# Two heads in each half of TensorE's rows for the scores, and the heads' sums spread by VectorE's shuffle

## The reference, cut to what matters

```python
x = conv3x3(quantize(x), sign(W) * mean|W|) + b
qkv = layernorm(x) @ wqkv + bqkv                 # per image 49 regions of 64 pixels
q_reg, k_reg = q.mean(pixels), k.mean(pixels)
idx = top_k(q_reg @ k_reg.T, 4)                  # 4 regions for each region
scores = q[region, head] @ k[idx, head].T * scale    # 8 heads of 8: 64 x 256
out = softmax(scores) @ v[idx, head]
x = x + out @ wo + bo
x = x + gelu(layernorm(x) @ w1 + bm1) @ w2 + bm2
```

## Time and profile before

| | |
|---|---|
| median of 3 runs | 5610.56 us (5608.67 to 5612.54) |
| the profiled execution's own time | 5625.85 us |
| its span, first to last instruction | 5623.2 us |
| mean granted TensorE clock | 0.898 |
| TensorE busy | 4720.9 us |
| VectorE busy | 3648.9 us |
| ScalarE busy | 3287.3 us |
| GpSimd busy | 2777.4 us |

### The profile page before, as it was taken

The page is one execution under the profiler, slowest core; times in us unless marked ns, Lnnn a source line. Parts: engine busy times, 40 slices in busy tenths (PEclk is TensorE's granted clock), DMA queues, the critical chain, the costliest instruction groups (busy, mean ns, idle before and its releaser), DMA issues.

```text
span 5623.2 us, 182695 instructions
## 1 busy us (share of the span) xinstructions
PE 4720.9 (84%) x43666; PEld 3049.9 (54%) x43666; DVE 3648.9 (65%) x8855; ACT 3287.3 (58%) x6282; POOL 2777.4 (49%) x9656
## 2 busy tenths in 40 slices
PE   2388888888889898888888889888888888888888
PEld 1265555655556555555555556555565655556564
DVE  2266666766667666676766667666676766667676
ACT  1156556565665756556565665656556565665657
POOL 1245455454554645455454554545455464554553
PEclk9589899988889989898989999989899998999989
DMA  2333343333423334243333423334233333423311
GB/s 61 95 99 92 82 109 75 94 84 91 108 68 102 82 93 103 72 109 83 96 87 89 109 69 101 82 94 104 71 110 88 94 84 92 111 65 106 83 45 33
DMA packets 626961, 494.05 MB, mean 88 GB/s; under 512 B 483792, under 2 KB 613968, under 8 KB 615536
## 3 DMA queue, kind: packets, MB, share of 16 engines
q10 hardware_dynamic: 335360, 212.04, 16.6%
q1 hardware_dynamic: 290416, 268.94, 16.5%
HBM read 268.80 MB, written 211.94 MB: 85 GB/s over the span
## 4 chain that ended last, share of the span: by engine, by line
PE 52%; DMA 13%; issue 9%; ACT 7%; DVE 6%; DVEq 4%; SPq 4%; ACTq 3%; POOL 2%; POOLq 0%
PE ps L1003 11%; PE ps L1033 9%; PE ps L1017 8%; DMA max_d<-tr 6%; PE ps L896 5%; DMA qm<-qk_d 3%; DVEq L223 3%; PE ps L953 3%; ACTq L237 2%; PE ps L989 2%; PE ps L916 2%; PE ps L912 2%; DMA xin<-in_x 2%; ACT pt L847 2%; PE ps L974 2%
## 5 line engine op out<-in xcount | busy, mean ns | idle before, releaser
L736 DVE TENSOR_REDUCE mx<-ps 128x4 f32<-128x1024 f32 x1568 | 1921.6, 1225 | 1396.2 <-PE ps L1003 1128.7
L847 ACT ACTIVATE pt<-ps 128x512 f32<-128x512 f32 x3136 | 1694.2, 592 | 875.0 <-PE ps L1017 811.9
L505 POOL COPY vg<-vs 64x72 f32 x6272 | 1563.5, 249 | 781.6 <-POOL kg L490 576.7
L1003 PE MATMUL ps<-kg,qm 96*128 96x256 f32 x6272 | 1358.3, 342 | 364.4 <-DVE mx L736 112.2
L490 POOL CAST kg<-ks 96x128 fp32r x3136 | 845.2, 295 | 1550.5 <-PE ps L1017 1195.5
L1003 PEld LDWEIGHTS ps<-kg,qm 96*128 96x128 f32 x6272 | 963.3, 206 | 1087.2 <-issue 889.0
L1017 PE MATMUL ps<-qm,kg 97*128 97x256 f32 x6272 | 1126.5, 303 | 151.7 <-ACT pt L847 96.9
L1033 PE MATMUL ps<-pt,vg 128*32 128x128 f32 x25088 | 1092.0, 294 | 51.8 <-DVE um L726 39.1
L1017 PEld LDWEIGHTS ps<-qm,kg 97*128 97x128 f32 x6272 | 940.2, 206 | 214.6 <-ACT pt L847 154.7
L1033 PEld LDWEIGHTS ps<-pt,vg 128*32 128x32 f32 x25088 | 629.5, 114 | 296.5 <-issue 58.0
L645 DVE CAST kg<-ks 96x128 fp32r x3136 | 630.9, 244 | 137.9 <-issue 132.4
(11 more groups left out here) (113 smaller groups left out, 4036.1 us busy)
## 6 DMA issues: line engine op xcount, KB each, us to landing
qk_d<-stg SPq DMA_DIRECT2D x224, 448.0 KB, 3.6
qm<-qk_d ACTq DMA_DIRECT2D x1792, 42.0 KB
ks<-qk_d ACTq DMA_DIRECT2D x96, 784.0 KB, 6.3
vs<-v_d ACTq DMA_DIRECT2D x64, 882.0 KB, 7.1
xin<-in_x SPq DMA_DIRECT2D x119, 224.0 KB, 2.6
xi_d<-xi SPq DMA_DIRECT2D x112, 224.0 KB, 2.7
qk_d<-stg SPq DMA_DIRECT2D x112, 224.0 KB, 3.2
max_d<-tr SPq DMA_DIRECT2D x1568, 2.0 KB
```

The source lines that it names most:

```text
L505: j = pool.tensor_copy(vg[slot][rows, (k // 2) * VW:(k // 2 + 1) * VW], vs[place(m)[0]][rows, bass.ds(region, 1), :].rearrange("p o n -> p ...
L736: v.tensor_reduce(mx[h % 2][:].rearrange("p (g j e) -> p g j e", g=2, j=2)[:, :, :, 0], ps[:, 0:2, :].rearrange("p g (j k) -> p g j k", j= ...
L847: act.activation(pt[m % 2][:, c], ps[:, 2 + c, :], ACT.Exp, scale=float(HD) ** -0.5).then_inc(S["pt_ready"], 1)
L1003: i = pe.matmul(ps[:, g, 256 * j:256 * j + 256], qm[c % 2][0:NP3, t, g, 2 * j:2 * j + 2, :].rearrange("p h t -> p (h t)"), kg[slot][0:NP3, ...
```

## The change

`qm` and `ks`, and so `kg`, hold the heads 0 and 1 of a group in partitions 0 to 47 and heads 2 and 3 in partitions 64 to 111; row 48 of each half takes the maxima. `scores` is now four products of 48 rows, two in each half of the rows of the array, and the result's bank is that of the half. `turned` is eight products of 49 rows and 128 columns instead of four of 97 rows and 256 columns; it waits for both exponentials of the step before ahead of the first, and signals at the last two. The -1 rows are filled in `ks` at the start and come with the copies; the gathers copy 128 partitions instead of 96. The keys are loaded by six transfers instead of three, and the loads (eight with those of the values, before five) go out in consecutive steps instead of every second one. `pick` and its product are gone: VectorE shuffles `um` into `rc` at offsets 0 and 1 (`SPREAD` gives for each of 32 rows the row to take), and ScalarE takes the logarithm from `rc` instead of a bank. The waits on banks 5 and 6 move from offset 0 to offsets 4 and 9.

```diff
@@ -28,9 +28,12 @@
 EPS = 1e-5
 HG = 4
 NG = HEADS // HG
-NP3 = 3 * HG * HD
+HALF = 64
+NP3 = 3 * 2 * HD
 VC = 18
 VW = 4 * VC
+
+SPREAD = [16] * HD + [17] * HD + [16] * 16
@@ -49,7 +52,7 @@
 ROUTE_AT = 62
 A_LOAD, B_LOAD = 70, 6
 QK_DMAS, V_DMAS = 3, 4
-KV_DMAS = 5
+KV_DMAS = 8
@@ -141,7 +143,7 @@
         ks = [sb(f"ks{i}", [128, NG, R, RT], F32R) for i in range(2)]
         vs = [sb(f"vs{i}", [128, R, VW]) for i in range(2)]
-        qm = [sb(f"qm{i}", [128, NW, NG, HG, RT], F32R) for i in range(2)]
+        qm = [sb(f"qm{i}", [128, NW, NG, 2, RT], F32R) for i in range(2)]
         kg = [sb(f"kg{i}", [128, NG, TOPK, RT], F32R) for i in range(RING)]
         vg = [sb(f"vg{i}", [128, 2 * VW + 16]) for i in range(RING)]
@@ -234,16 +236,18 @@
             i, s = c // NW, c % NW
             src = qk_d[bass.ds(q, 1), i, 0:C, :, ST * s:ST * s + ST].rearrange("o (g h d) q (s t) -> g h (o d q) s t", g=NG, h=HG, s=NW)
             for g, h in heads:
-                eng.dma_start(qm[c % 2][24 * h:24 * h + 24, :, g, h, :].bitcast(F32), src[g, h]).then_inc(q_loaded[c % 2], 16)
+                row = HALF * (h // 2) + 24 * (h % 2)
+                eng.dma_start(qm[c % 2][row:row + 24, :, g, h % 2, :].bitcast(F32), src[g, h]).then_inc(q_loaded[c % 2], 16)
         def keys_values(eng, q, i, n):
-            if n < 3:
-                src = qk_d[bass.ds(q, 1), i, C:2 * C, n // 2, :].rearrange("o (g c) n -> (o c) g n", g=NG)
-                dst = ks[i][n:NP3:3].rearrange("p g r t -> p g (r t)").bitcast(F32)
+            if n < 6:
+                part, term = n // 3, n % 3
+                src = qk_d[bass.ds(q, 1), i, C:2 * C, term // 2, :].rearrange("o (g j c) n -> j (o c) g n", g=NG, j=2)[part]
+                dst = ks[i][HALF * part + term:HALF * part + NP3:3].rearrange("p g r t -> p g (r t)").bitcast(F32)
             else:
                 src = v_d[bass.ds(q, 1), i].rearrange("o t r n -> (o t) (r n)")
-                dst = vs[i][64 * (n - 3):64 * (n - 3) + 64].rearrange("p r n -> p (r n)")
+                dst = vs[i][64 * (n - 6):64 * (n - 6) + 64].rearrange("p r n -> p (r n)")
             eng.dma_start(dst, src).then_inc(kv_loaded[i], 16)
@@ -259,14 +263,14 @@
                 if h == A_LOAD:
                     staged_all(eng, p + 1)
                     gathered(eng, p, R)
-                if 0 <= h - A_LOAD < 2 * KV_DMAS and (h - A_LOAD) % 2 == 0:
-                    keys_values(eng, p + 1, 0, (h - A_LOAD) // 2)
+                if 0 <= h - A_LOAD < KV_DMAS:
+                    keys_values(eng, p + 1, 0, h - A_LOAD)
             local = h if kind == "lead" else h - STEPS
             if local >= 0 and kind != "last":
                 if local == B_LOAD and kind != "lead":
                     gathered(eng, p, STEPS)
-                if 0 <= local - B_LOAD < 2 * KV_DMAS and (local - B_LOAD) % 2 == 0:
-                    keys_values(eng, p if kind == "lead" else p + 1, 1, (local - B_LOAD) // 2)
+                if 0 <= local - B_LOAD < KV_DMAS:
+                    keys_values(eng, p if kind == "lead" else p + 1, 1, local - B_LOAD)
         def first_loads(eng):
@@ -361,8 +365,8 @@
                     sp.wait_ge(hopped[m % 2], (p * R + m // 2 + 1) * 16)
                     settled(sp)
-                    sp.dma_start(qm[m // NW % 2][NP3:NP3 + 1, m % NW].rearrange("o g h t -> o (g h t)").bitcast(F32),
-                                 max_d[m % RING].rearrange("j p -> (j p)").unsqueeze(0)).then_inc(row_ready[m % RING], 16)
+                    sp.dma_start(qm[m // NW % 2][NP3:128:HALF, m % NW].rearrange("o g e t -> o (g e t)").bitcast(F32),
+                                 max_d[m % RING].rearrange("(j g) p -> j (g p)", j=2)).then_inc(row_ready[m % RING], 16)
                 if live(h, kind):
...
@@ -487,8 +485,8 @@
                     pool.wait_ge(kv_loaded[i], (p + m // STEPS + 1) * (16 * KV_DMAS))
                     settled(pool)
                 for k, region in enumerate(chosen(m, 2)):
-                    j = pool.tensor_copy(kg[slot][0:NP3, :, 2 + k, :],
-                                         ks[place(m)[0]][0:NP3, :, bass.ds(region, 1), :].rearrange("p g o t -> p g (o t)"))
+                    j = pool.tensor_copy(kg[slot][:, :, 2 + k, :],
+                                         ks[place(m)[0]][:, :, bass.ds(region, 1), :].rearrange("p g o t -> p g (o t)"))
                 j.then_inc(S["kp_ready"], 1)
@@ -589,8 +587,8 @@
                 v.memset(t[:], 1.0)
             for t in qm:
                 v.memset(t[:].rearrange("p s g h t -> p (s g h t)").bitcast(F32), 0.0)
-            for t in kg:
-                v.memset(t[:].rearrange("p g k t -> p (g k t)").bitcast(F32), -1.0)
+            for t in ks:
+                v.memset(t[:].rearrange("p g r t -> p (g r t)").bitcast(F32), -1.0)
             link(v.memset(rx[:], 0.0))
             v.memset(epst, EPS)
@@ -642,8 +640,8 @@
                     settled(v)
                 gather_ready(v, p, m)
                 for k, region in enumerate(regions(v, regs, m, 0, 2)):
-                    j = v.tensor_copy(kg[slot][0:NP3, :, k, :],
-                                      ks[place(m)[0]][0:NP3, :, bass.ds(region, 1), :].rearrange("p g o t -> p g (o t)"))
+                    j = v.tensor_copy(kg[slot][:, :, k, :],
+                                      ks[place(m)[0]][:, :, bass.ds(region, 1), :].rearrange("p g o t -> p g (o t)"))
                 j.then_inc(S["kd_ready"], 1)
@@ -696,6 +694,11 @@
                 for s, off in f_item(h):
                     n = p * NW + s
                     b = s % 2
+                    if off in (0, 1):
+                        if off == 0:
+                            v.wait_ge(S["um_ready"], p * (4 * 14) + (NW + s + 1) * 4)
+                            settled(v)
+                        v.stream_shuffle(rc[:, off], um0[:, s] if off == 0 else um1[:, b], SPREAD).then_inc(S["sum_full"], 1)
                     if off in (2, 3):
                         i = off - 2
@@ -802,7 +805,7 @@
                     if off in (1, 2):
                         i = off - 1
                         act.wait_ge(S["sum_full"], n * 2 + i + 1)
-                        act.activation(rc[:, i], ps[:, 5 + i, 0:ST], ACT.Ln).then_inc(S["lns_ready"], 1)
+                        act.activation(rc[:, i], rc[:, i], ACT.Ln).then_inc(S["lns_ready"], 1)
                         act.wait_ge(S["lns_ready"], n * 2 + i + 1)
                         act.activation(rc[:, i], rc[:, i], ACT.Exp, scale=-1.0).then_inc(S["rcs_ready"], 1)
@@ -921,8 +924,6 @@
                 if h == ROUTE_AT:
                     pe.wait_ge(S["rx_ready"], q * NW + NW)
                     pe.wait_ge(S["l_ready"], q * (2 * NW) + 2 * NW)
-                    if not first:
-                        pe.wait_ge(S["lns_ready"], p * (2 * NW) + 1)
                     settled(pe)
                     for i in range(2):
@@ -940,21 +941,13 @@
                 for s, off in f_item(h):
                     n = p * NW + s
-                    if off == 0:
-                        pe.wait_ge(S["um_ready"], p * (4 * 14) + (NW + s + 1) * 4)
-                        if s >= 2:
-                            pe.wait_ge(S["ot_ready"], 1 + n - 1)
-                        elif kind == "loop":
-                            pe.wait_ge(S["l_ready"], (p + 2) * (2 * NW))
-                            pe.wait_ge(S["v_ready"], (p + 2) * NW)
-                        if s:
-                            pe.wait_ge(S["lnv2_ready"], n)
-                        for i, src in enumerate((um0[:, s], um1[:, s % 2])):
-                            pe.matmul(ps[:, 5 + i, 0:ST], pick[:], src, start=True, stop=True).then_inc(S["sum_full"], 1)
                     if off == 4:
                         pe.wait_ge(S["un_ready"], n * 2 + 2)
                         if s:
                             pe.wait_ge(S["z_ready"], n * 2)
+                        elif kind == "loop":
+                            pe.wait_ge(S["l_ready"], (p + 2) * (2 * NW))
+                            pe.wait_ge(S["v_ready"], (p + 2) * NW)
                         for i in range(2):
                             j = pe.matmul(ps[64 * i:64 * i + 64, 6, 0:ST], wo[:], rc[:, i], start=True, stop=True)
@@ -977,8 +970,9 @@
                         pe.matmul(ps[:, 6, 0:ST], mean_w[:], st2[:], start=True, stop=True).then_inc(S["var2_full"], 1)
                     if off == 9:
                         pe.wait_ge(S["nm2_ready"], n + 1)
-                        if s < NW - 1:
-                            pe.wait_ge(S["lns_ready"], n * 2 + 4)
+                        pe.wait_ge(S["ot_ready"], 1 + n)
+                        if s == 0 and kind == "loop":
+                            pe.wait_ge(S["lg_ready"], p + 2)
                         for i in range(2):
                             d = slice(64 * i, 64 * i + 64)
@@ -1000,9 +994,9 @@
                     pe.wait_ge(S["mx_ready"], T)
                 for g in range(NG):
                     for j in range(2):
```

(23 more changed lines are left out.)

13 lines of the change are left out of this document (3 added, 10 removed).

## The result

The changed kernel took **6002.18 us** (median of 4 runs, 5973.57 to 6031.92) beside 5611.55 us for the kernel before on the same chip: a ratio of 1.0692, 95% interval 1.0637 to 1.0746. It is slower by 6.9%. The forecast was 5645 us with a range of 5410 to 5830 us: the sign was right and the size far off. The profiled execution took 5973.57 us, with a span of 5971.7 us and a mean clock of 0.771 (0.898 before).

What follows compares the result with a forecast made beforehand. It took a ring of waits, scores, maximum, scores, as the bound, with no engine full. Gains of 204 us against 240 us of clock loss gave 5662 us profiled, so 5645 us predicted (+0.6%), range 5410 to 5830 us.

Steps and rivals of the forecast that it cites:

- a fall of the clock: TensorE drops to the lower clock after a less busy stretch; over two steps 3.2 us, of which 2.4 uncovered.
- the halves with their clock: Half-array products on TensorE: scores 0.24 us shorter per step, more at the lower clock, against a clock loss of 240 us.
- the late exponentials: Both exponentials start after all eight turned products; where ScalarE is late this costs 0.2 us, once per finishing cycle.
- finishing cycle: Steps that finish a strip, in a pattern repeating every 7 steps, 112 times over 16 pairs; forecast gain 0.16 us each.
- The eight loads: Loads of keys and values, eight instead of five with the same bytes: no time, covered by ScalarE's 42% idle.
- shuffle for the product: Two VectorE shuffles of 0.60 us replace TensorE's 1.77 us pick product per strip; VectorE ends last, so nothing of 1.77 is left.
- start: At the kernel's start, changed fills and the fills of the key ring together add 4 us.
- The clock, +240 us: Half of the finishing cycles and four tenths of the others fall once more: 112 x 0.9 x 2.4 us.
- The slot falls from 0.21 to about 0.12 us, 0.37 us less in a step: Turned products at the lower clock: time per product shrinks with half the columns; no gain at the upper clock.
- the -90 us: About 250 steps already at the lower clock save 0.80 us instead of 0.24, two thirds of the difference on the path.
- near 0.80: Sign that the forecast is right: TensorE's mean granted clock, 0.898 in the kernel before.
- TensorE's busy time: Sign that the forecast is right: total busy time of TensorE near 4300 us.

Runs made afterwards that it cites:

- all_but_halves: Kernel before with the shuffle, maxima written to two rows, turned products behind both exponentials and eight loads, without the array's halves: 5862.91 us, 1.0417.
- loads_spaced: Changed kernel with each pair of half loads of keys and values issued in one step, every second step: 5976.08 us, 1.0616.
- shuffle_only: Kernel before with only the product with pick replaced by VectorE's shuffles: 5572.87 us, 0.9912.
- late_exponentials: shuffle_only with full-height turned products that start behind both exponentials of the step before and give both signals at their end: 5682.57 us, 1.0095.
- one_row_and_fill: Changed kernel without the second half's row of maxima, with added TensorE products whose result nobody reads: 5750.22 us, 1.0238.
- split_on_sync: Changed kernel with the maxima written by two one-row transfers on SyncE's queue in place of one two-row transfer: 6078.13 us, 1.0812.

## Why the prediction was wrong

Three steps of the prediction failed most. It had no term for the row of maxima that becomes two (166 us, measured in full height). It priced a fall of the clock at 2.4 us, so that the halves with their clock came to about nothing (measured 154 us slower). And it took the late exponentials for 0.2 us once in a finishing cycle (22 us, measured 103 us). The eight loads, put at no time, cost 43 us.

The parts in order, in us against 5611.55; "measured" is the difference of two ratios of runs that differ in that part alone.

| part | forecast | measured |
|---|---|---|
| shuffle for the product | +13 | -49 |
| second row of maxima | not named | +166 |
| late exponentials | +22 | +103 |
| eight loads | 0 | +43 |
| these four together (all_but_halves) | +36 | +234 |
| the halves with their clock | about -4 | +154 |
| start | +4 | not taken apart |
| sum | +36 | +388 |

(The forecast's split: of a finishing cycle's 0.16 us, 0.48 is the scores, 0.2 the late exponentials; the rest, 0.12 x 112, is what the shuffle would cost.) The four parts measured one by one give 263 us, and together 234 us: their waits cover each other a little. And the 166 us are of full height with 4 KB; taken out of the changed kernel, the second row gives back 56 us, and 95 us with the idle products.

**The transfer that wasn't costed.** The largest single part has no term in the prediction. The change part by part left out that L364's one destination row becomes two. The line is in the diff, its duration was in the trace of before (0.23 us), and beside it stood a transfer to 16 partitions with 0.54 us in the same queue. These two were the bounds: up to 0.3 us in each of 1568 steps, some 490 us if all of it showed, on a chain of which `max_d<-tr` already held 6%.

**"Eight loads ... no time, covered by ScalarE's 42% idle".** The cover was looked for on the engine that issues. What grew is the wait for the maxima's transfer: from 251 to 310 us, and the longest from 4.3 to 10.2 us, in the full-height kernel that differs by these loads alone. The run changed three things at once, eight transfers for five, half the partitions in each of the key loads, and no step's pause between them. loads_spaced, which gives back the pause alone, took the longest wait from 10.5 to 6.6 us; that points at the pause and doesn't prove it.

**"This costs 0.2 us, once per finishing cycle".** The mechanism was right and the count was wrong: the prediction priced only the step in which ScalarE is late and TensorE waits. That wait did double (104 to 200 us in the waits of shuffle_only and late_exponentials), but the larger part is the other way round, ScalarE's wait for the turned products, in 920 steps for 633 and 324 us longer. 103 us over 1568 steps are 0.07 us a step, and five times the term.

**The clock, +240 us.** The number of falls came out near, 161 before and 257 after, 96 more where the prediction had 112 x 0.9; but that was luck. The prediction laid the falls to the work that the halves and the lost product take from TensorE. By the clock records the product's loss alone adds 8 (shuffle_only 169), the late exponentials bring it to 212, and all_but_halves has 234. The halves add only 23. What they do is make the stretches at the lower level longer: 6.9 us in the mean in all_but_halves, 10.6 in the changed kernel. So the price of a fall was too low. It was taken as two steps of 1.2 us; in the longer stretches the strips' products are slow too. The low time grew by 92 us a pair, 69 of them with the halves; 0.9 x 112 falls of the six us in the earlier trace rows would give 38.

**"The slot falls from 0.21 to about 0.12 us, 0.37 us less in a step"** (turned products at the lower clock). It doesn't: the eight take 0.94 us, and 0.11 us is the gain, for in the kernel before the four full-height ones took 1.05 us:

```profile
2568.33 1.05 PE L1017 MATMUL ps<-qm,kg 97*128 97x256 f32 x4
```

The prediction took the slot from the scores (0.21 us) and doesn't show this row. The gain of 0.80 us for a step at the lower clock becomes 0.53 (1.22 to 0.80 for the scores, and this 0.11), and the -90 us that were drawn with it shrink in the same way.

**The shuffle: right where it was costed, and one place missed.** In an ordinary cycle VectorE is what ends last, as forecast: 101 of 111 maxima behind a first shuffle and 97 of 111 behind a second start less than 0.1 us after VectorE's instruction before them. In the timeline, at the lower clock (the records of two instructions of VectorE that follow each other overlap by some 0.1 us):

```profile
2644.68 0.65 DVE L701 STREAM_SHUFFLE rc<-um 128x448 f32<-128x448 f32 x1
2645.22 1.22 DVE L739 TENSOR_REDUCE mx<-ps 128x4 f32<-128x1024 f32 x1
...
2646.75 0.66 DVE L701 STREAM_SHUFFLE rc<-um 128x448 f32<-128x448 f32 x1
...
2648.04 1.22 DVE L739 TENSOR_REDUCE mx<-ps 128x4 f32<-128x1024 f32 x1
```

The gain of 49 us comes from one step of each pair. The first finishing step, 60, took 7.15 us as a mean of pairs 2 to 13 of the kernel before, and takes 2.64 us in shuffle_only: 4.5 us in each of 16 pairs are 72 us, and everything else together lost some 20, where the term said 13. That the term's size was near is partly luck, since the clock of shuffle_only also fell, from 0.898 to 0.886. In the timeline of before, at that step:

```profile
2817.01 0.74 DVE L667 COPY vstg<-ps 128x384 f32<-128x384 f32 x2
...
2817.80 3.35 PE L953 MATMUL ps<-um,pick 128*128 128x448 f32 x4 [3.04 <-DVE vstg L667]
```

The product needed banks 5 and 6, which held the last strip's values until VectorE had copied them, and TensorE stood 3.04 us behind that wait and came back at the lower clock. A shuffle writes no bank. The prediction read one cycle and multiplied by 112; the pair's first one isn't like the others.

**What was right.** The halves run at once (0.50 us for 0.71). The turned products stay at 0.57 to 0.66 us at the upper clock, and their eight weight loads take 0.54 of the 0.57 us, which fits that the loads set the pace. A shuffle takes 0.65 us; 0.60 was taken, and the estimate by proportion from the Trainium skill (VectorE: DVE Perf Modes, the perf-mode tier table) was 0.53: the row decides, and both were low. The mean clock is 0.771 for "near 0.80". Not right was TensorE's busy time: 4740 us where 4300 was forecast, since it wasn't raised by the clock forecast beside it. On the drain at a change of the array's shape (the Trainium skill, TensorEngine Tiling (Array Packing), Key Properties) no run here tells anything: none changes the count of shape changes alone.

**What stays open.** one_row_and_fill, with queue and clock treated, is 1.4 points above late_exponentials. Eight loads account for about 0.8, the idle products' own time may be the rest; this wasn't taken apart. Why split_on_sync is slower than the changed kernel isn't known. Whether key loads in halves with a step's pause between all of them would be free wasn't tried. No version here beats the shuffle alone by more than the measurement can tell.

## What to carry to other kernels

Price each line of a diff, the transfers first: one more destination partition doubled the issue in a queue that every step goes through, and cost 1 to 3% here. A change that makes the busiest engine's products shorter, where that engine isn't full, can lose more through its clock than it saves. To find out, add idle products: if more work makes the kernel faster and the granted clock rises, it was the clock. And when several small parts ride along with a large one, put all but the large one into the old kernel: that single run showed that 60% of the loss came with what the idea brought along, and not with the halves themselves. Last, a count that comes out as forecast isn't yet a cause confirmed: most of the 96 new falls of the clock were there without the halves.

## What the runs showed of the hardware

- The issue of these transfers on SyncE's queue goes by whether one partition or more take part, rather than by the bytes: 2 KB to one partition 0.23 us, 2 KB to two 0.50 us, 4 KB to two 0.59 us, 2 KB from 16 partitions 0.54 us; 1 KB to one partition 0.23 to 0.24 us. The same 1 KB issued by GpSimd took 0.48 us.
- Half-height products of 128 columns with 128-column weights run at 0.57 us for eight when the halves take turns, at 0.67 us when the four of a half come together. Their weight loads take 0.54 and 0.64 us.
- 377 us of added products made a kernel of 6002 us 160 us shorter, and its mean clock went from 0.771 to 0.839.
- The mean stretch at the lower clock was 6.9 us with the scores in full height (all_but_halves) and 10.6 us in halves, at 234 and 257 falls.
